# Reordering the head, the block change and the last group of a two-layer feed-forward kernel

## The chip, the cores and the metric

The kernel runs on one core of one Trainium2 chip. The metric is the device time of one execution in microseconds (us). The times given are those of three runs.

## What is computed

```python
# x: (4, 512, 512) = 2048 tokens of 512 values, all float32
# layer 1 (weights 1376 x 512), keeps the larger half of |silu(gate)| of every token
s = silu(ln(x) @ w_gate.T)
s[the 688 smallest |s| of each row] = 0
x = x + ln((s * (ln(x) @ w_up.T)) @ w_down.T)
# layer 2, the same without the selection
x = x + ln((silu(ln(x) @ W_gate.T) * (ln(x) @ W_up.T)) @ W_down.T)
```

`ln` is a layer norm without scale and shift.

## The kernel before

The kernel is written with one instruction list for each engine; the order within a list is fixed by hand and engines wait for each other through semaphores only. TensorE (PE) multiplies, ScalarE (ACT), VectorE (DVE) and GpSimd (POOL) do the rest, and SyncE (SP) issues all DMAs.

**Precision.** Every matrix product is made of three matmuls. Each operand is split into a rounded part `hi` (made by ScalarE, `split_..._hi`) and the rest `lo` (made by VectorE, `split_..._lo`); the three are hi x lo, lo x hi and hi x hi.

**First block (layer 1).** The 2048 tokens are 16 tiles of 128. For tile j PE makes three gate products of 460 columns (`product(j, 0, n)`), three up products (`product(j, 1, n)`), each of 12 matmuls, and later the down product `down(j)` of 11 chunks of h, 33 matmuls of 512 columns, in three groups of chunks (4, 4, 3: `TG`), for each of which it waits for its part of the split h (`hlo_done`). The gate and up products rotate through five, later seven PSUM banks. A bank is free for the next product when ScalarE's `silu(j, n)` (gate) or VectorE's `times_up(j, n)` (up) has read it.

**Selection.** Between silu and the down product of a tile stands a chain over four engines: VectorE takes absolute values (`abs_values`), ScalarE counts six times how many exceed a threshold (`count(j, 0)` to `count(j, 5)`), GpSimd moves the threshold after each of the first five (`newton`), VectorE looks for the exact limit (`find_below`, `find_top`, `find_flag`), masks (`select`) and turns h (`swap_h`), a DMA of four parts moves it (`move_h`), then `split_h_hi` on ScalarE and `split_h_lo` on VectorE split it in three groups each. `down(j - 2)` stands among the products of tile j. `y_stats`, `y_rstd` (GpSimd), `normalise_y` (ScalarE) and `add_residual` (VectorE) finish a tile.

**Weights of the first block** come in 18 pieces (`PIECES`): 6 of gate, 6 of up (number 11 is the second half of the third up product), 6 of down with two chunks each (numbers 12 to 17). ScalarE and VectorE split each (`split_weights_hi`, `split_weights_lo`). `wlo_done` counts the pieces that are done; `NP` is 18 and `GU_PIECES` is 12.

**Second block (layer 2).** The tokens are four groups of four tiles (`GROUPS`, `GT`). Products are turned: `chunk(g, j, m)` makes gate (m = 0) or up (m = 1) of 128 rows of the hidden layer for 512 tokens, 12 matmuls, for 11 chunks j (`JC`). The weights are loaded into the buffers of the first block in pairs of chunks (`split_pair_hi`, `split_pair_lo`); the first pair of gate and that of up serve chunks 0 and 1. `down2(g, j, tiles)` adds chunk j to the y of the given tiles, 3 matmuls for each tile, and each of the four tiles has its own bank. In the last group `down2` of the last three chunks stands behind the last `chunk`.

The lists meet at these places, all of which the change touches: PE's `down`, the chunks of the block change (line 622) and the last group (lines 636 to 647); ScalarE's list of the head (lines 779 to 786) and its tile loop (line 813); VectorE's tile loop (line 1170) and its last lines (1270 to 1274).

Of the kernel before, what the change touches and what calls it, by code (L numbers as in the profile page):

```python
# [16 lines left out]
def sandwich(nc, x, x_first, w_gate, w_up, w_down, W_gate, W_up, W_down, out):  # L17
# [5 lines left out]
    JC = -(-I // P)  # L23
# [8 lines left out]
    GT = 4  # L32
    GROUPS = TILES // GT
# [64 lines left out]
    with ctx:  # L98
# [375 lines left out]
        def _(pe):  # L474
# [46 lines left out]
            def down(j):  # L521
                if j >= 1:
                    pe.wait_ge(res_done, j)
                if j == 0:
                    pe.wait_ge(wlo_done, NP)
                    pe.wait_ge(xlo_done, 4)
                for g, (c0, cn) in enumerate(TG):
                    pe.wait_ge(hlo_done, 3 * j + g + 1)
                    for c in range(c0, c0 + cn):
                        hhi, hlo = (hT[:, s, c * P:(c + 1) * P] for s in range(2))  # L530
                        for i, (h, w) in enumerate(((hhi, down_lo), (hlo, down_hi), (hhi, down_hi))):
                            last = nc.tensor.matmul(y_ps[:, :], h, w[:, c, :],  # L532
                                                    start=(c == 0 and i == 0),
                                                    stop=(c == JC - 1 and i == 2))
                last.then_inc(y_done, 1)

            def chunk(g, j, m):

                idx = g * JC + j
                what = ("gu"[m], idx, 0)  # L540
                bank_free(what)
                if g == 0:
                    pe.wait_ge(plo_done, P_AT[m * NPAIR + j // 2])
                if j == 0 and m == 0:
                    pe.wait_ge(xlo_done, POS[TILES + GT * g + GT - 1] + 1)
                dst = bank(what)
                k = width(j)
                xt = x_group(g)
                for c in range(KC):
                    at = j * KC * P + c * k  # L550
                    hi, lo = gu_hi[m][:, at:at + k], gu_lo[m][:, at:at + k]
                    for i, (w, s) in enumerate(((lo, 0), (hi, 1), (hi, 0))):
                        last = nc.tensor.matmul(dst[0:k, :], w, xt[:, s, c, :],  # L553
                                                start=(c == 0 and i == 0), stop=(c == KC - 1 and i == 2))
                last.then_inc((g2_done, u2_done)[m], 1)
# [63 lines left out]
                    if n == max(6 - j, 0) and j < TILES - 1:  # L619
                        down(j - 2)  # L620
            down(TILES - 3)
            for j in range(2):
                chunk(0, j, 0)
                chunk(0, j, 1)
            down(TILES - 2)
            for j in range(2, 4):
                chunk(0, j, 0)
# [7 lines left out]
            for g in range(GROUPS):  # L635
                for j in range(6 if g == 0 else 0, JC):
                    chunk(g, j, 0)
                    chunk(g, j, 1)
                    if g > 0 and j == 0:
                        down2(g - 1, JC - 1, range(GT))  # L640
                    if j >= 2:
                        down2(g, j - 2, range(GT))
                if g < GROUPS - 1:
                    down2(g, JC - 2, range(GT))
            for r in range(GT):
                down2(GROUPS - 1, JC - 2, (r,), last_tile=False)
                down2(GROUPS - 1, JC - 1, (r,))

        @block.scalar
        def _(act):  # L650
            def split_weights_hi(w):
                m, n, c = PIECES[w]
                slot = w % NSLOT
                act.wait_ge(stage_in[slot], 16 * (w // NSLOT + 1))
                if m < 2:
                    src = stage[:, slot, :, 0:CW[n]]
                    dst = gu_hi[m][:, :].rearrange("p (c i) -> p c i", c=KC)[:, c:c + 2, CO[n]:CO[n] + CW[n]]
                else:
                    src, dst = stage[:, slot, 0:c, :], down_hi[:, n:n + c, :]
                nc.scalar.activation(dst, src, ACT.Copy).then_inc(whi_done, 1)  # L660
# [35 lines left out]
            def silu(j, n):  # L696
                act.wait_ge(g_done, G_AT[j, n])
                if j >= 2:
                    act.wait_ge(h_moved, 64 * (j - 1))
                nc.scalar.activation(prod[:, j % 2, CO[n]:CO[n] + CW[n]], bank(("G", j, n))[:, 0:CW[n]],  # L700
                                     ACT.Silu).then_inc(silu_done, 1)
# [77 lines left out]
            silu(1, 1)  # L779
            split_weights_hi(10)  # L780
            silu(1, 2)
            count(0, 2)
            split_weights_hi(11)
            count(0, 3)
            split_weights_hi(12)
            count(0, 4)
# [24 lines left out]
            split_x_hi(4)  # L811
            split_h_hi(1)
            for j in range(3, TILES - 1):
                count(j - 1, 5)
                silu(j, 0)
                if j > 3:
                    split_h_hi(j - 2)
                silu(j, 1)
                silu(j, 2)
                if j - 1 in TWO:  # L820
                    split_x_hi(TILES + j - 1 - TWO[0])
                if 4 < j < TWO[0]:
                    split_x_hi(j + 1)
                guess(j)
                for n in range(3):
                    count(j, n)
                if j in TWO:
                    split_x_hi(j + 1)
                count(j, 3)
                normalise_y(j - 2)  # L830
                count(j, 4)
                if j == 3:
                    split_x_hi(5)
# [61 lines left out]
        def _(dve):  # L895
# [274 lines left out]
            for j in range(3, TILES - 1):  # L1170
                a = XSEQ[POS[j + 1]:]
                find_below(j - 1)
                find_top(j - 1)
                if j > 3:
                    split_h_lo(j - 2)
                abs_values(j)
                if j - 1 in TWO:
                    split_x_lo(TILES + j - 1 - TWO[0])
                if 4 < j < TWO[0]:
                    split_x_lo(j + 1)  # L1180
                if j > 3:
                    x_stats(a[1])
                find_flag(j - 1)
                select(j - 1)
                if j > 3:
                    x_normalise(a[1])
                swap_h(j - 1)
                if j in TWO:
                    split_x_lo(j + 1)
                    x_stats(a[2])  # L1190
                y_stats(j - 2)
                times_up(j, 0)
                if j in TWO:
                    x_normalise(a[2])
                add_residual(j - 2)
                times_up(j, 1)
                times_up(j, 2)
                if j == 3:
                    split_x_lo(5)
            last = TILES - 1  # L1200
# [43 lines left out]
            for g in range(GROUPS):  # L1244
                for j in range(4 if g == 0 else 0, JC):
# [18 lines left out]
                    if g < GROUPS - 1:  # L1264
                        if j in X_AT:
                            split_x_lo(a + X_AT[j])
                        if j + 1 in X_AT:
                            x_stats(a + X_AT[j + 1])
                            x_normalise(a + X_AT[j + 1])
            for r in range(GT):  # L1270
                y_stats(XT2 - GT + r)
                if r:
                    add_residual(XT2 - GT + r - 1)
            add_residual(XT2 - 1)

        @block.gpsimd
# [147 lines left out]
```

## Time and profile before

| | us |
|---|---|
| median of three runs (749.35 to 749.54) | 749.38 |
| the profiled execution | 748.73 |
| its span in the trace | 746.9 |
| PE busy | 733.0 |
| VectorE busy | 448.0 |
| ScalarE busy | 345.9 |
| GpSimd busy | 133.2 |

Times in the trace count from the start of the span. TensorE's granted clock was 0.997 of full speed over the span. In the order of time of an engine a line gives the start, the length, the engine, the line of the kernel, the operation, what it writes and reads, how many like instructions are merged in the line, and in brackets the idle time of the engine before it with what ended it. Matmuls overlap, so the length of one is more than the distance to the next. "L969" is VectorE's split of h, "L918" its split of a weight piece, "L1007" `times_up`, "L930" its split of a pair, "L1101" and "L1108" the product and the split of h in the second block.

### The profile page before, as it was taken

Reading aid. Unit: us, or ns where it says so; the run is one execution under the profiler, and the core shown is the slowest. Engines: PE = TensorE matmul, PEld = TensorE weight load, DVE = VectorE, ACT = ScalarE, POOL = GpSimd, SP = SyncE. Lnnn points to the kernel's source line nnn. Section 1 sums busy time; section 2 is a strip of 40 time slices with the busy share of each in tenths; the row PEclk is TensorE's granted clock in tenths of the full one; section 3 lists DMA queues with packets and bytes.
Section 4 is the critical chain, followed back from the end, with each engine's and each line's share of the span. In section 5 each row is a group of like instructions: output and inputs, shape, how many; then the busy total and the mean of one; then the engine's idle time right before and its main releaser. Section 6 shows DMA issues by size and latency. Waiting matters only on the chain.

```text
span 746.9 us, 9447 instructions
## 1 busy us (share of the span) xinstructions
PE 733.0 (98%) x3309; PEld 615.7 (82%) x3309; DVE 448.0 (60%) x865; ACT 345.9 (46%) x575; POOL 133.2 (18%) x278
## 2 busy tenths in 40 slices
PE   8999999999999999999999999999999999999996
PEld 7888878888888888888788887888878888788884
DVE  7788778888787788887876452533316333151214
ACT  6786676776666676667735221311113112131112
POOL 0432123233322223332210000100001000010001
PEclk9999999999999999999999999999999999999998
DMA  8532235544335554557726112111112122030001
GB/s 285 185 88 69 64 105 134 132 109 89 110 96 133 147 113 103 126 143 215 269 74 204 32 29 57 73 41 29 33 53 85 28 37 34 15 134 8 1 1 56
DMA packets 88610, 69.85 MB, mean 94 GB/s; under 512 B 60368, under 2 KB 72144, under 8 KB 88368
## 3 DMA queue, kind: packets, MB, share of 16 engines
q1 hardware_dynamic: 88560, 69.23, 34.0%
q8 instruction: 26, 0.43, 0.2%
q14 instruction: 24, 0.20, 0.1%
HBM read 42.21 MB, written 16.84 MB: 79 GB/s over the span
## 4 chain that ended last, share of the span: by engine, by line
PE 68%; DVE 11%; issue 9%; POOL 5%; ACT 5%; DMA 1%; DVEq 0%; POOLq 0%; SPq 0%; ACTq 0%
PE gu_ps L553 32%; PE tr_ps L574 12%; PE y_ps L532 8%; PE gu_ps L517 7%; PE tr_ps L517 5%; PE y_ps L574 4%; ACT junk L688 3%; POOL move L1319 2%; POOL thr L1322 2%; DVE below L1051 2%; DVE hT L969 2%; DVE top L1056 1%; DVE xstat L937 1%; DVE absv L1000 1%; DMA xin<-in_x_first 1%
## 5 line engine op out<-in xcount | busy, mean ns | idle before, releaser
L688 ACT ACTIVATE junk<-absv,thr 128x1383 bf16<-128x1383 f32 x96 | 139.2, 1450 | 52.3 <-POOL thr L1322 51.6
L1101 DVE TENSOR_TENSOR prod<-gu_ps,prod 128x512 f32<-128x512 f32 (+1 forms) x44 | 30.3, 689 | 166.8 <-PE gu_ps L553 166.5
L532 PE MATMUL y_ps<-down_hi,hT 128*128 128x512 f32 x352 | 109.0, 391 | 0.0
L741 ACT ACTIVATE prod<-gu_ps 128x512 f32<-128x512 f32 (+1 forms) x44 | 26.2, 595 | 132.1 <-PE gu_ps L553 132.1
L532 PEld LDWEIGHTS y_ps<-down_hi,hT 128*128 128x128 f32 x352 | 66.1, 188 | 14.4
L532 PE MATMUL y_ps<-down_lo,hT 128*128 128x512 f32 x176 | 69.5, 395 | 1.6 <-DVE hT L969 1.1
L517 PE MATMUL gu_ps<-up_hi,xT 128*128 128x460 f32 (+1 forms) x240 | 69.5, 371 | 0.0
L517 PE MATMUL gu_ps<-gate_hi,xT 128*128 128x460 f32 (+1 forms) x232 | 67.2, 371 | 0.0
L1319 POOL TENSOR_SCALAR move<-sgn 128x1 f32<-128x1 f32 x80 | 40.1, 502 | 94.0 <-ACT junk L688 93.8
L1303 POOL TENSOR_TENSOR yrstd<-yvar,half 128x1 f32<-128x1 f32 x32 | 18.7, 583 | 208.1 <-DVE yvar L978 207.2
L553 PE MATMUL gu_ps<-xg_odd,gate_hi 128*128 128x512 f32 (+1 forms) x176 | 54.4, 390 | 0.0
L553 PE MATMUL gu_ps<-xg_even,gate_hi 128*128 128x512 f32 (+1 forms) x176 | 54.3, 390 | 0.0
L553 PE MATMUL gu_ps<-xg_even,up_hi 128*128 128x512 f32 (+1 forms) x176 | 54.3, 390 | 0.0
L553 PE MATMUL gu_ps<-xg_odd,up_hi 128*128 128x512 f32 (+1 forms) x176 | 54.3, 389 | 0.0
L1296 POOL TENSOR_TENSOR xrstd<-xvar,half 128x1 f32<-128x1 f32 x32 | 19.1, 595 | 187.3 <-DVE xvar L941 187.3
L517 PEld LDWEIGHTS gu_ps<-up_hi,xT 128*128 128x128 f32 x240 | 45.1, 188 | 5.2
L517 PEld LDWEIGHTS gu_ps<-gate_hi,xT 128*128 128x128 f32 x232 | 43.6, 188 | 4.9
L517 PE MATMUL gu_ps<-up_lo,xT 128*128 128x460 f32 (+1 forms) x120 | 44.8, 373 | 0.5 <-DVE prod L1007 0.5
L755 ACT ACTIVATE xT<-prod 128x512 fp32r<-128x512 f32 (+1 forms) x22 | 13.9, 632 | 67.1 <-DVE prod L1101 63.6
L517 PE MATMUL gu_ps<-gate_lo,xT 128*128 128x460 f32 (+1 forms) x116 | 43.4, 374 | 0.7 <-DVE gate_lo L918 0.4
L517 PE MATMUL tr_ps<-gate_hi,xT 128*128 128x460 f32 (+1 forms) x152 | 44.1, 371 | 0.0
L517 PE MATMUL tr_ps<-up_hi,xT 128*128 128x460 f32 (+1 forms) x144 | 41.7, 371 | 0.0
(137 smaller groups left out, 1527.2 us busy)
## 6 DMA issues: line engine op xcount, KB each, us to landing
absv<-prod SPq DMA_DIRECT2D x64, 176.0 KB, 3.4
xin<-x_scratch SPq DMA_DIRECT2D x18, 256.0 KB, 2.7
xres<-in_L_attn_x SPq DMA_DIRECT2D x16, 256.0 KB, 5.2
x_scratch<-xres SPq DMA_DIRECT2D x16, 256.0 KB, 2.8
xres<-x_scratch SPq DMA_DIRECT2D x14, 256.0 KB, 2.8
out<-xres SPq DMA_DIRECT2D x14, 256.0 KB, 2.1
xin<-in_L_attn_x SPq DMA_DIRECT2D x11, 256.0 KB, 3.5
xT<-xin SPq DMA_DIRECT2D x44, 64.0 KB, 2.5
```

Source lines behind the costliest of these rows:

```text
L517: last = nc.tensor.matmul(dst[:, 0:CW[n]], xt, w, start=(c == 0 and i == 0), stop=(c == KC - 1 and i == 2))
L532: last = nc.tensor.matmul(y_ps[:, :], h, w[:, c, :], start=(c == 0 and i == 0), stop=(c == JC - 1 and i == 2))
L553: last = nc.tensor.matmul(dst[0:k, :], w, xt[:, s, c, :], start=(c == 0 and i == 0), stop=(c == KC - 1 and i == 2))
L574: last = nc.tensor.matmul(y_bank(b)[:, :], h[0:k, toks], w[0:k, j, :], start=(j == 0 and i == 0), stop=(j == JC - 1 and i == 2))
L688: nc.scalar.activation(junk[:, 0:I + PAD], absv[:, q, A0 - PAD:A0 + I], ACT.Sign, bias=thr[:, q:q + 1], scale=-1.0, accum_out=sgn[:, q:q + ...
L741: nc.scalar.activation(prod[0:k, 0, 0:GW], bank(("g", idx, 0))[0:k, :], ACT.Silu).then_inc(s2_done, 1)
L969: nc.vector.tensor_tensor(lo, raw, hi.bitcast(F32), ALU.subtract).then_inc(hlo_done, 1)
L1051: nc.vector.scalar_tensor_tensor(below[:, :], values(q), thr[:, q:q + 1], values(q), ALU.is_le, ALU.mult).then_inc(below_done, 1)
L1101: nc.vector.tensor_tensor(prod[0:k, 0, GW:2 * GW], bank(("u", idx, 0))[0:k, :], prod[0:k, 0, 0:GW], ALU.mult).then_inc(p2_done, 1)
L1296: nc.gpsimd.tensor_tensor(xrstd[:, :], xvar[:, :], half[:, :], ALU.pow).then_inc(xr_done, 1)
L1303: nc.gpsimd.tensor_tensor(yrstd[:, q:q + 1], yvar[:, q:q + 1], half[:, :], ALU.pow).then_inc(yr_done, 1)
L1319: stepped(nc.gpsimd.tensor_scalar(move[:, :], sgn[:, q:q + 1], sgn[:, q:q + 1], float((WINDOW - 1) ** 2) + 0.5, ALU.mult, ALU.is_gt))
```

## The change

It moves work and removes or adds none, but for the waits of one product.

- `down(0)` waits for the weight pieces of each group of chunks instead of for all 18 at its start.
- At the change of blocks PE makes gate 0, gate 1, up 0, up 1 instead of gate 0, up 0, gate 1, up 1.
- In the last group, behind the last chunk, PE makes chunks 8 and 9 of tiles 0 and 1, then chunk 10 of tiles 0 and 1, then all three of tile 2 and all three of tile 3. Before, it made chunk 8 of all four tiles and then chunks 9 and 10 tile by tile.
- In the head ScalarE splits weight piece 11 ahead of the third count of tile 0.
- In the loop's tiles 4 to 10 ScalarE's `split_h_hi(j - 2)` stands ahead of the sixth count of tile j - 1, and VectorE's `split_h_lo(j - 2)` ahead of `find_top(j - 1)`. For tiles 11 on nothing moves.
- In the loop's tiles 3 to 5 VectorE's `add_residual(j - 2)` stands behind the third `times_up(j, n)` instead of the first.
- At the end VectorE takes the statistics of tiles 0, 1 and 2 before the first residual add, and those of tile 3 behind it.

```diff
                 if j == 0:
-                    pe.wait_ge(wlo_done, NP)
                     pe.wait_ge(xlo_done, 4)
                 for g, (c0, cn) in enumerate(TG):
+                    if j == 0:
+                        pe.wait_ge(wlo_done, GU_PIECES + (c0 + cn + 1) // 2)
...
             down(TILES - 3)
-            for j in range(2):
-                chunk(0, j, 0)
-                chunk(0, j, 1)
+            for m in range(2):
+                chunk(0, 0, m)
+                chunk(0, 1, m)
...
-                    if j >= 2:
+                    if j >= 2 and (g, j) != (GROUPS - 1, JC - 1):
                         down2(g, j - 2, range(GT))
...
-            for r in range(GT):
-                down2(GROUPS - 1, JC - 2, (r,), last_tile=False)
-                down2(GROUPS - 1, JC - 1, (r,))
+
+            for r, chunks in ((0, 2), (1, 2), (0, 1), (1, 1), (2, 3), (3, 3)):
+                for j in range(JC - 3, JC - 1) if chunks > 1 else ():
+                    down2(GROUPS - 1, j, (r,), last_tile=False)
+                if chunks != 2:
+                    down2(GROUPS - 1, JC - 1, (r,))
...
             silu(1, 2)
+            split_weights_hi(11)
             count(0, 2)
-            split_weights_hi(11)
             count(0, 3)
...
             for j in range(3, TILES - 1):
+                if 3 < j < TWO[0]:
+                    split_h_hi(j - 2)
                 count(j - 1, 5)
                 silu(j, 0)
-                if j > 3:
+                if j >= TWO[0]:
                     split_h_hi(j - 2)
...
                 find_below(j - 1)
+                if 3 < j < TWO[0]:
+                    split_h_lo(j - 2)
                 find_top(j - 1)
-                if j > 3:
+                if j >= TWO[0]:
                     split_h_lo(j - 2)
...
-                add_residual(j - 2)
+                if j > 5:
+                    add_residual(j - 2)
                 times_up(j, 1)
                 times_up(j, 2)
+                if j <= 5:
+                    add_residual(j - 2)
...
-            for r in range(GT):
-                y_stats(XT2 - GT + r)
-                if r:
-                    add_residual(XT2 - GT + r - 1)
+            y_stats(XT2 - 4)
+            y_stats(XT2 - 3)
+            y_stats(XT2 - 2)
+            add_residual(XT2 - 4)
+            y_stats(XT2 - 1)
+            add_residual(XT2 - 3)
+            add_residual(XT2 - 2)
             add_residual(XT2 - 1)
```

## Rows read from the trace of the kernel before

**Rows 1.** The page's first section: busy time, share and instructions of each engine.
```profile
PE 733.0 (98%) x3309; PEld 615.7 (82%) x3309; DVE 448.0 (60%) x865; ACT 345.9 (46%) x575; POOL 133.2 (18%) x278
```
**Rows 2.** Waits of PE: engine, tile, line, releaser: us in total, times, longest.
```profile
PE y_ps L532 <- DVE hT L969: 1.1, 3, 0.6
```
**Rows 3.** PE in order of time, tiles 0 to 6 of the first block.
```profile
33.04 0.58 PE L517 MATMUL tr_ps<-up_hi,xT 128*128 128x456 f32 x2
34.35 0.47 PE L517 MATMUL tr_ps<-up_lo,xT 128*128 128x456 f32 x1 [0.73 <-DVE up_lo L918]
...
56.68 0.37 PE L517 MATMUL tr_ps<-gate_lo,xT 128*128 128x460 f32 x1
...
59.88 0.50 PE L532 MATMUL y_ps<-down_lo,hT 128*128 128x512 f32 x1 [0.52 <-DVE down_lo L918]
...
80.53 0.43 PE L532 MATMUL y_ps<-down_lo,hT 128*128 128x512 f32 x1
...
98.89 0.48 PE L517 MATMUL gu_ps<-up_lo,xT 128*128 128x460 f32 x1 [0.54 <-DVE prod L1007]
...
104.46 0.47 PE L532 MATMUL y_ps<-down_lo,hT 128*128 128x512 f32 x1 [0.28 <-DVE hT L969]
...
145.97 0.47 PE L532 MATMUL y_ps<-down_lo,hT 128*128 128x512 f32 x1 [0.61 <-DVE hT L969]
```
**Rows 4.** Order of time at the change of blocks, PE and VectorE.
```profile
365.67 0.47 PE L553 MATMUL gu_ps<-xg_even,up_lo 128*128 128x512 f32 x1 [0.67 <-DVE up_lo L930]
...
390.28 1.28 DVE L969 TENSOR_TENSOR hT<-absv,hT 128x512 fp32r<-128x512 f32 x2
...
392.37 0.39 PE L532 MATMUL y_ps<-down_lo,hT 128*128 128x512 f32 x1
```
**Rows 5.** Order of time of the last group, PE, VectorE and SyncE.
```profile
732.98 0.69 DVE L1108 TENSOR_TENSOR hT<-prod,hT 96x512 fp32r<-96x512 f32 x1 [0.70 <-ACT hT L755]
...
739.30 0.63 PE L574 MATMUL y_ps<-down_hi,hT 96*128 96x512 f32 x2
...
741.02 0.69 DVE L974 BATCH_NORM_STATS2 ystat<-y_ps 128x6 f32<-128x512 f32 x1
...
744.27 0.81 SPq L373 DMA_DIRECT2D out<-xin  x2
```
**Rows 6.** Order of time of the head, GpSimd, ScalarE and VectorE.
```profile
27.64 2.76 POOL L1322 TENSOR_SCALAR thr<-move,step,thr 128x1 f32<-128x1 f32 x1
...
32.06 0.29 POOL L1319 TENSOR_SCALAR move<-sgn 128x1 f32<-128x1 f32 x1 [1.67 <-ACT junk L688]
...
32.47 0.34 POOL L1322 TENSOR_SCALAR thr<-move,step,thr 128x1 f32<-128x1 f32 x1
33.06 1.44 ACT L688 ACTIVATE junk<-absv,thr 128x1383 bf16<-128x1383 f32 x1
33.19 1.11 DVE L918 TENSOR_TENSOR up_lo<-stage,up_hi 128x912 fp32r<-128x912 f32 x1 [2.29 <-ACT up_hi L660]
```
**Rows 7.** Order of time of tiles 2 to 6, ScalarE and VectorE.
```profile
55.66 0.56 ACT L700 ACTIVATE prod<-tr_ps 128x460 f32<-128x460 f32 x1 [2.35 <-DMA absv<-prod]
...
79.66 1.75 DVE L969 TENSOR_TENSOR hT<-absv,hT 128x512 fp32r<-128x512 f32 x3
...
97.60 0.69 DVE L993 TENSOR_TENSOR xres<-y_ps,xres 128x512 f32<-128x512 f32 x1 [2.44 <-ACT y_ps L727]
98.21 1.17 DVE L1007 TENSOR_TENSOR prod<-gu_ps,prod 128x460 f32<-128x460 f32 x2
...
141.96 1.65 DVE L1051 SCALAR_TENSOR_TENSOR below<-absv,thr 128x1376 f32<-128x1376 f32 x1 [0.46 <-POOL thr L1322]
...
145.15 1.74 DVE L969 TENSOR_TENSOR hT<-absv,hT 128x512 fp32r<-128x512 f32 x3
```
**Rows 8.** The page's DMA issues: tiles, count, KB each, us from issue to landing.
```profile
absv<-prod SPq DMA_DIRECT2D x64, 176.0 KB, 3.4
xin<-x_scratch SPq DMA_DIRECT2D x18, 256.0 KB, 2.7
xres<-in_L_attn_x SPq DMA_DIRECT2D x16, 256.0 KB, 5.2
```

## The prediction before the run

> **What bounds the kernel now.** I read the page first: TensorE (PE) is busy 733.0 of 746.9 us [rows 1]. So only two things can be shortened by a change that removes no work: the idle time of PE, and what runs before its first and after its last matmul. The waits view of PE lists nine kinds of wait, 6.9 us in all; the largest after the start is the down product waiting for the split of h, 1.1 us in three waits [rows 2]. PE's own order of time then gives the place of each. A wait costs more than the idle figure, so I measure it as the start of the matmul against the start it would have had: matmuls of 460 columns start 0.21 us apart and those of 512 columns 0.23, and the first one after a wait takes 0.47 instead of 0.37 us, 0.10 more. The row pair at 33.04 and 34.35 us [rows 3] gives 34.35 - (33.04 + 0.42) = 0.89, and with the restart 0.99 us. In the same way: first down product at 59.88, 0.69 + 0.10; second up product of tile 4 at 98.89, 0.71 + 0.10; down products of tiles 2, 3 and 4 at 104.46, 125.06 and 145.97, 0.45, 0.36 and 0.78, each + 0.10 (the first and the last of the three stand there); the first up chunk of the second block at 365.67, 0.84 + 0.10 [rows 3, 4]. After 366 us PE waits for nothing that counts, until the tail: the last matmul ends at 739.93, the statistics of its tile start at 741.02, and the last two stores are issued from 744.27 on [rows 5].
>
> **Who is behind PE.** Most of the early waits are ends of one chain that PE does not drive: ScalarE counts, GpSimd moves the threshold, VectorE selects and turns h, a DMA moves it, ScalarE and VectorE split it. I call it the selection chain. A wait on PE that is removed only helps until PE next meets this chain; so I follow PE from gate to gate, with the gain G that it has against before.
>
> **Head: the split of piece 11 ahead of the third count.** That count waits for the threshold that GpSimd delivers at 27.64 + 2.76 = 30.40 [rows 6], and the change puts the 0.95 us split into this idle time, so it costs nothing on ScalarE. VectorE's half (1.11 us, at 33.19) has 2.29 us of idle time before it, so it can start at 33.19 - 2.29 = 30.90 and is done about 31.95 instead of 34.30 [rows 6]. PE's third up product wants it at 33.46: the wait is gone, G = 0.99. The fourth count no longer stands behind the split: it started at 33.06 and its threshold was ready at 32.47 + 0.34 = 32.81, so it can start at about 32.85 [rows 6]. The whole selection chain moves 0.21 us forward.
>
> **Gate 1, tile 3's first gate product.** It was at 56.68 without a wait; its bank is freed by the silu at 55.66, 0.56 long, which waits for the DMA that moves h [rows 3, 7]. With G = 0.99 PE wants the bank at 55.69, and the silu ends at 56.22 - 0.21 = 56.01. A new wait of about 0.4 us with restart: G falls to about 0.5.
>
> **Gate 2, the first down product.** Its first four chunks need pieces 12 and 13 of down and the first part of split h, both done at about 58; the piece it waited for, which VectorE finished just before 59.88 [rows 3], is now asked for with the last chunks, 5.5 us later. The wait of 0.79 goes: G = 1.3. Nothing is queued behind the two waits that the change adds on PE but its own matmuls, and their semaphores are long up.
>
> **Gate 3, the second down product.** It started at 80.53 [rows 3], and the first of the three splits it needs ends about 0.7 after 79.66, at 80.35 [rows 7]. It had no slack at all. The change reorders nothing here, so this gate moves by the chain's 0.21 only, less a restart: G = 0.15. Nearly all that the head and the first down product gave is handed back. This is the step that a sum of removed waits would miss.
>
> **Tile 4's up product.** The residual add of tile 1 waited for the normalised y with 2.44 us idle, and the two VectorE products behind it at 98.21 held PE's bank [rows 7]. With the add behind them they need not wait and PE has its bank: 0.81 more, G = 0.96. The add itself still ends near 98.1, with the next down product 5 us away.
>
> **Down products of tiles 2, 3 and 4.** Before, VectorE did below (1.65), top, then the split, which started 3.19 us after below (141.96, 145.15) [rows 7]. Now the split comes between, 1.6 us sooner, if ScalarE's half is there. That half now stands ahead of the sixth count; it takes 1.56 us and waits for the h DMA, whose last part lands about 3.4 to 3.9 us after its issue [rows 8], which is 0.5 us after ScalarE comes free in tiles 5 and 6. It pushes the sixth count and the first silu back by some 1.6 to 2.1 us; the third silu ends where VectorE is done with top, within 0.1 us, so abs and the next count start no later (chain at -0.47 to -0.52, since below, split, top and abs now follow without VectorE's small gaps). Then, by the same steps in VectorE's order of time: down 2 is ready at 102.6 and wanted at 103.06 (104.02 without its wait, less 0.96), G = 1.5. Down 3 is ready at 122.9 and wanted at 123.2, G = 1.96. Down 4: below starts at 141.96 - 0.47, the first split ends at 143.73, PE starts 0.14 later at 143.87; it would have wanted 143.23. One wait of 0.64 stays, and G = 145.97 - 143.87 = **2.10**. The three down products stand (145.97 - 104.46) / 2 = 20.8 us apart because the chain sets them; a tile of PE is 72 x 0.21 + 33 x 0.23 = 22.7. From down 5 on, behind whole tiles, PE does not meet the chain again, and from tile 9 the third silu waits for PE, so the chain follows at -2.1. Bounds for this part: 1.6 if the chain does not move at all (only the reorder counts), 2.7 if the last wait goes too.
>
> **Change of blocks.** Gate chunk 0, gate chunk 1, up chunk 0, up chunk 1: the up weights are wanted 2.7 us later than before, and they were 0.84 late [rows 4]. Gate chunk 1 needs the same pair of gate weights as chunk 0 and a bank that was freed by a silu of the last tile, long before. Total **0.94**. What is next: the split of h for down 15. It starts at 390.28, its first part takes 0.68 and PE takes it up 0.14 later, at 391.1; PE asked at 392.37 and will ask at 391.44 [rows 4]. It keeps 0.3 us of cover. Bounds 0.8 to 0.94.
>
> **Tail.** In the last group PE does two chunks of two tiles first, then their last chunks, then tile 2 and tile 3 with three chunks each; twelve groups of 0.70 us as before. The last chunk's h is split at 732.98 + 0.69 = 733.67 [rows 5] and is now wanted at 734.2 instead of 734.9: 0.5 us of cover is left where it was 1.2. Tile 2 ends at 737.8 instead of 738.5, and VectorE does its statistics (1.1), the add of tile 0, and is free at 739.6, before the last matmul's end at 739.93. The last statistics start at 739.97 instead of 741.02: 1.05 earlier, and GpSimd, ScalarE and the two half adds follow (the other adds fit before the half add at 742.8). The stores come closer together: those of tiles 1 and 2 and the two halves would be issued about 0.6, 0.9 and 0.4 us apart, where each of the halves was clear of the others before. I take **1.0**, bounds 0.5 (transfers get in each other's way) to 1.05.
>
> **Sum.** 2.10 + 0.94 + 1.0 = 4.04 us. The profiled execution took 748.73 with a span of 746.9, so it would go to 744.7 and 742.9; the median of the runs shown is 749.38, so **745.3**.
>
> **Rivals.** (a) Every wait goes and nothing is late next: 0.99 + 0.79 + 0.81 + 0.55 + 0.46 + 0.88 + 0.94 + 1.05 = 6.5, 742.9. Against it stands gate 3 without slack. 6%. (b) The selection chain does not move or gets longer by about 1 us, and the tail gives half: GpSimd's operation took 2.76 us where its like take 0.34, under two VectorE operations that read SBUF [rows 6]. Should the moved split (to 31.95) overlap the next one at 32.06, the chain loses up to 1.1 us: 4.04 - 1.1 = 2.9, down to 2.0 with the tail at 0.5 less and a little more waiting, 746.5 to 747.4. 20%. The Trainium skill (GPSIMD Engine Reference, Specifications) says that the SBUF interfaces are shared with VectorE and that instructions with two SBUF inputs contend; by that rule this edit is safe only by the 0.1 us between the two, and the time would be 746.4. (c) The change doesn't do what it says: down 2 to 4 are late by the DMA instead of by the order and the tail is held by the stores; gain under 1.5, about 748.5. 8%. (d) Slower: ScalarE's half of the split, now ahead of the sixth count, waits for the h DMA in tiles 4 to 10. If this lands 2 us later than now in tiles 4 to 6 (the residual load needs 5.2 us to land where this one needs 3.4 [rows 8]), sixth count, silus and abs of each tile slip by 2 us, three times 2 against the 4 gained: about 751. It decides from 1.9 us of delay on; now it is 0.5. 4%. The forecast has 62%.
>
> **Range and chances.** The forecast's own bounds are 1.6 + 0.8 + 0.5 = 2.9 to 2.7 + 0.94 + 1.05 = 4.7, 744.7 to 746.5; with most of (b) and half of (a) the range is 743.7 to 747.0. 0.2% (1.5 us) is about what can be told from no change: faster by more 0.88, within 0.08, slower 0.04.
>
> **What would show it.** Right: no wait at 33, 59, 98, 103 and 123 us; new small waits near 56 and 80; one of 0.6 left before down 4; none at 364; span near 742.9; last statistics 0.05 us after the last matmul. Wrong: PE's gain at down 1 much over 0.2 would mean that the chain moved more than I think; a longer idle time of PE at down 4 than 0.8, that ScalarE's new order lengthens the chain; a long GpSimd operation at 32 us, rival (b).

## The result and the profile after

The changed kernel takes 745.11 us (median of four runs, 744.72 to 745.35) against 749.37 before (749.35 to 749.54): 4.26 us less, ratio 0.9942 with an interval of 0.993 to 0.9953. Forecast were 745.3 us and a gain of 4.04. The interval allows a gain of 3.5 to 5.2 us, so that the two agree to 0.2 us is closer than the runs can tell. The profiled execution of after is its slowest, 745.35, with a span of 743.5.

The first section of the page, then the waits of PE (us in total, times, longest):

```profile
span 743.5 us, 9449 instructions
PE 731.9 (98%) x3309; PEld 616.0 (83%) x3309; DVE 446.9 (60%) x865; ACT 345.0 (46%) x575; POOL 132.7 (18%) x278
```
```profile
PE y_ps L533 <- DVE hT L975: 1.2, 2, 1.0
PE tr_ps L517 <- ACT prod L704: 0.7, 1, 0.7
```

Busy times are those of before [rows 1] to within 1.1 us. The three waits of the down products [rows 2] have become two, and a wait for a silu is new. PE's own order of time gives their places:

```profile
56.91 0.48 PE L517 MATMUL tr_ps<-gate_lo,xT 128*128 128x460 f32 x1 [0.72 <-ACT prod L704]
...
81.20 0.47 PE L533 MATMUL y_ps<-down_lo,hT 128*128 128x512 f32 x1 [0.98 <-DVE hT L975]
...
98.90 0.37 PE L517 MATMUL gu_ps<-up_lo,xT 128*128 128x460 f32 x1
...
103.92 0.39 PE L533 MATMUL y_ps<-down_lo,hT 128*128 128x512 f32 x1
...
124.06 0.40 PE L533 MATMUL y_ps<-down_lo,hT 128*128 128x512 f32 x1
...
144.56 0.47 PE L533 MATMUL y_ps<-down_lo,hT 128*128 128x512 f32 x1 [0.22 <-DVE hT L975]
...
366.13 0.39 PE L554 MATMUL gu_ps<-xg_even,up_lo 128*128 128x512 f32 x1
```

The brackets at 34, 59, 98, 104, 125 (0.21) and 365 us of before [rows 3, 4] are gone. Those at 56.91 and 81.20 stand where the forecast put new ones, and a small one stays ahead of the fifth down product (down 4). Where the residual add was moved, VectorE now does it at 98.30, behind both products. VectorE's split of h (L975) follows `below` directly, and ScalarE's half stands ahead of the sixth count and waits for its DMA:

```profile
121.97 1.57 ACT L725 ACTIVATE hT<-absv 128x512 fp32r<-128x512 f32 x3 [1.12 <-DMA absv<-prod]
```
```profile
142.16 1.65 DVE L1057 SCALAR_TENSOR_TENSOR below<-absv,thr 128x1376 f32<-128x1376 f32 x1 [1.54 <-POOL thr L1336]
143.72 1.75 DVE L975 TENSOR_TENSOR hT<-absv,hT 128x512 fp32r<-128x512 f32 x3
```

The tail of after; it answers to [rows 5]:

```profile
736.92 0.62 PE L575 MATMUL y_ps<-down_hi,hT 96*128 96x512 f32 x2
737.25 2.42 SPq L368 DMA_DIRECT2D out<-xres  x2
...
737.58 0.70 DVE L980 BATCH_NORM_STATS2 ystat<-y_ps 128x6 f32<-128x512 f32 x1 [0.36 <-PE y_ps L575]
...
739.92 0.33 SPq L368 DMA_DIRECT2D out<-xin  x1
...
740.83 0.83 SPq L373 DMA_DIRECT2D out<-xin  x2
```

The last matmul ends at 737.54 (736.92 + 0.62), 2.39 earlier than before, and the last statistics start 0.04 behind it. The span is shorter by 3.4, so 1.0 comes from behind the last matmul. These 3.4 are less than the 4.26 of the medians; the next part of the trace tells why.

**The head, where the two profiled executions differ.** GpSimd and ScalarE of after, then VectorE's statistics of x tile 3 in before, after and the first experiment:

```profile
26.79 1.36 POOL L1310 TENSOR_TENSOR xrstd<-xvar,half 128x1 f32<-128x1 f32 x1 [2.44 <-DVE xvar L947]
28.14 0.29 POOL L1333 TENSOR_SCALAR move<-sgn 128x1 f32<-128x1 f32 x1
28.54 2.76 POOL L1336 TENSOR_SCALAR thr<-move,step,thr 128x1 f32<-128x1 f32 x1
32.97 0.29 POOL L1333 TENSOR_SCALAR move<-sgn 128x1 f32<-128x1 f32 x1 [1.67 <-ACT junk L692]
```
```profile
31.34 1.45 ACT L692 ACTIVATE junk<-absv,thr 128x1383 bf16<-128x1383 f32 x1 [2.49 <-POOL thr L1336]
...
33.75 1.45 ACT L692 ACTIVATE junk<-absv,thr 128x1383 bf16<-128x1383 f32 x1 [0.55 <-POOL thr L1336]
```
```profile
24.69 0.70 DVE L937 BATCH_NORM_STATS2 xstat<-xin 128x6 f32<-128x512 f32 x1 [0.90 <-DMA xin<-in_x_first]
```
```profile
25.61 0.69 DVE L943 BATCH_NORM_STATS2 xstat<-xin 128x6 f32<-128x512 f32 x1 [1.47 <-DMA xin<-in_x_first]
```
```profile
26.10 0.69 DVE L938 BATCH_NORM_STATS2 xstat<-xin 128x6 f32<-128x512 f32 x1 [1.93 <-DMA xin<-in_x_first]
```

The same x tile lands 0.92 later in after. Its reciprocal root stands in GpSimd's list ahead of the second threshold step, which thus runs at 28.54 instead of 27.64 [rows 6]. In all nine profiled kernels with this order of the head (24.69 to 26.10 for the statistics) the step starts 2.93 to 2.95 us behind them. The third count follows at 31.34 and the whole selection chain runs 0.7 later than in the trace of before (0.9, less the 0.2 that the new order gives). The change did not cause this: the first experiment below, an execution of 749.93 us where its median is 749.21, shows still more of it. Over the nine kernels the time of the profiled execution less the kernel's median rises, on the whole, with the start of these statistics: -0.64 and -0.55 us at 24.69 and 24.96, 0.03 at 25.45, 0.24 and 0.72 at 25.61 and 26.10. The execution of before on which the forecast was made (748.73) was likewise an early one against its median of 749.38.

### The profile page after: what moved, and what is told of

The parts are those of the page before. It is cut to its first block, busy times and chain, and to the rows that moved or that the text cites. A ratio compares the mean times of both kernels' runs of the same rounds, so it can differ in the third digit from the quotient of the medians.

```text
span 743.5 us, 9449 instructions
## 1 busy us (share of the span) xinstructions
PE 731.9 (98%) x3309; PEld 616.0 (83%) x3309; DVE 446.9 (60%) x865; ACT 345.0 (46%) x575; POOL 132.7 (18%) x278
## 4 chain that ended last, share of the span: by engine, by line
PE 80%; issue 6%; DVE 5%; ACT 4%; POOL 3%; DMA 1%; SPq 0%; DVEq 0%; POOLq 0%; ACTq 0%
PE gu_ps L554 32%; PE tr_ps L575 12%; PE y_ps L533 12%; PE gu_ps L517 11%; PE tr_ps L517 8%; PE y_ps L575 4%; ACT junk L692 2%; POOL move L1333 1%; POOL thr L1336 1%; DVE below L1057 1%; DVE hT L975 1%; DVE absv L1006 1%; DMA absv<-prod 1%; POOL xrstd L1310 0%; DVE xstat L943 0%
```

## Experiments

Each kernel was timed in five rounds beside the kernel before on the same chip. The edits are made to the kernel before unless the heading says another.

**The split of piece 11 ahead of the third count, and the first down product's waits, alone.**

```diff
-                    pe.wait_ge(wlo_done, NP)
+                        pe.wait_ge(wlo_done, GU_PIECES + (c0 + cn + 1) // 2)
...
+            split_weights_hi(11)
             count(0, 2)
-            split_weights_hi(11)
```


> Only the two edits of the head: the split of piece 11 ahead of the third count, and the down product of tile 0 that waits for its own pieces. Theory of the gates (prediction): both waits of PE go (0.99 and 0.79 us), but the second down product had no slack behind the selection chain, so 0.15 to 0.25 us are left of it at 80 us, and the waits at 98 to 146 us come back as they were: gain 0.2 us, ratio 0.9997. Rival, sum of removed waits: 1.8 us, ratio 0.9976.

749.21 against 749.41 us, ratio 0.9997 (0.9988 to 1.0006). Both waits are gone from the trace, and two others, longer ones, stand further on:

```profile
57.50 0.48 PE L517 MATMUL tr_ps<-gate_lo,xT 128*128 128x460 f32 x1 [1.30 <-ACT prod L701]
...
81.71 0.47 PE L533 MATMUL y_ps<-down_lo,hT 128*128 128x512 f32 x1 [0.92 <-DVE hT L970]
```

Two removed waits of 0.99 and 0.79 us are worth 0.2 us, by the interval at most 0.9: PE runs up against the selection chain. The reading by gates holds, the sum of waits (1.8) does not.

**The moved splits of h and residual adds, alone.**

```diff
+                if 3 < j < TWO[0]:
+                    split_h_hi(j - 2)
                 count(j - 1, 5)
...
+                if 3 < j < TWO[0]:
+                    split_h_lo(j - 2)
                 find_top(j - 1)
...
+                if j <= 5:
+                    add_residual(j - 2)
```


> Only the edits of tiles 3 to 10: h is split ahead of the sixth count and of top, and the residual add of tiles 1 to 3 goes behind the third product. Gates: the down product of tile 4 is set by the selection chain, whose split comes 1.6 us sooner, and the chain gains 0.3 from VectorE's small gaps: gain 1.9 us, ratio 0.9975; PE's wait before the down product of tile 3 or 4 does not vanish. Rival, sum of removed waits: 0.81 + 0.55 + 0.46 + 0.88 = 2.7 us. Rival (d), the chain gets longer by the wait for the DMA: no gain or a loss.

747.47 against 749.41, ratio 0.9973 (0.9961 to 0.9984). As by the gates: the waits at 34 and 59 us are there (34.62, 60.16), those from 98 to 125 are not, and before down 4, at 144.14, 0.39 is left without the restart (idle 0.22).

**The order of the first two chunks, alone.**

```diff
-            for j in range(2):
-                chunk(0, j, 0)
-                chunk(0, j, 1)
+            for m in range(2):
+                chunk(0, 0, m)
+                chunk(0, 1, m)
```


> Only the new order of the first four chunks of the second block. All theories: 0.94 us, ratio 0.9987, and no wait of PE near 364 us. If a wait before the down product of tile 15 or the first down product of the second block takes it back, the gain is 0.3 us or less.

748.43 against 749.41, ratio 0.9987 (0.9978 to 0.9996): the 0.94 of the forecast.

**The last group, alone** (PE's part and VectorE's as in the change; the lines show where each begins to differ).

```diff
+            for r, chunks in ((0, 2), (1, 2), (0, 1), (1, 1), (2, 3), (3, 3)):
...
+            y_stats(XT2 - 2)
+            add_residual(XT2 - 4)
+            y_stats(XT2 - 1)
```


> Only the last group: PE's order and VectorE's. Prediction: the last statistics start 0.05 us after the last matmul instead of 1.1, gain 1.0 us, ratio 0.9987. Rival, stores in each other's way: 0.5 us, with the last store landing over 2 us after its issue.

748.62 against 749.41, ratio 0.9989 (0.998 to 0.9999): 0.8 where 1.0 was forecast, and the interval holds both. The four parts alone give 0.2 + 1.94 + 0.98 + 0.79 = 3.9 of the 4.26.

**The last group, only VectorE's order.**

```diff
-            for r in range(GT):
-                y_stats(XT2 - GT + r)
...
+            y_stats(XT2 - 2)
+            add_residual(XT2 - 4)
+            y_stats(XT2 - 1)
```


> The kernel before with VectorE's order at the end alone (statistics of tile 2 ahead of the first residual add), PE's order as before. Tile 2 ends at 738.5, its statistics take 1.1, the add of tile 0 0.7, so the last statistics start at 740.3 instead of 741.0: gain 0.7 us of the tail's 1.05, ratio 0.9991. If VectorE's order does nothing without PE's: 0.

748.73 against 749.52, ratio 0.9991 (0.9982 to 1.0). VectorE's order alone brings about what the whole part did (0.79 each). In the traces the last statistics start 1.09 us behind the last matmul in before, 0.29 with VectorE's order and 0.03 with both; that last 0.26 is below what these intervals tell.

**Only the residual adds, and only the splits of h** (the two halves of the second experiment).

```diff
-                add_residual(j - 2)
+                if j > 5:
+                    add_residual(j - 2)
                 times_up(j, 1)
                 times_up(j, 2)
+                if j <= 5:
+                    add_residual(j - 2)
```


> Only the residual adds of tiles 1 to 3 behind the third product. PE's wait at 98.9 us (0.81) goes, but the down product of tile 2 is set by the chain and comes when it came before, about 0.1 us sooner at most: gain 0.1 to 0.2 us, ratio 0.9998. Sum of removed waits: 0.8 us, 0.9989.

749.52 against 749.61, ratio 1.0001 (0.9991 to 1.001).

```profile
98.90 0.37 PE L517 MATMUL gu_ps<-up_lo,xT 128*128 128x460 f32 x1
...
105.22 0.47 PE L532 MATMUL y_ps<-down_lo,hT 128*128 128x512 f32 x1 [1.14 <-DVE hT L969]
```

The wait at 98 us is gone, and the down product 6 us on waits 1.14 instead of 0.28 [rows 3]: a removed wait of 0.81 is worth nothing by itself.

```diff
+                if 3 < j < TWO[0]:
+                    split_h_hi(j - 2)
                 count(j - 1, 5)
...
+                if 3 < j < TWO[0]:
+                    split_h_lo(j - 2)
                 find_top(j - 1)
```


> Only the split of h ahead of the sixth count and of top in tiles 4 to 10. The down products of tiles 2 to 4 have their data 1.6 us sooner each; PE's wait at 98.9 us stays, and so PE wants down 4 at 145.2 less the waits at 104 and 125 (0.55, 0.46), 144.2, while the chain offers it at 144.2: gain 1.7 us, ratio 0.9977. Together with the residual edit 2.0 were measured; a sum of both parts alone of 2.0 or less would agree.

747.73 against 749.61, ratio 0.9973 (0.9962 to 0.9983).

```profile
99.71 0.48 PE L517 MATMUL gu_ps<-up_lo,xT 128*128 128x460 f32 x1 [0.59 <-DVE prod L1009]
...
145.06 0.39 PE L532 MATMUL y_ps<-down_lo,hT 128*128 128x512 f32 x1
```

Nearly the whole gain of the tiles is this one edit, because it moves the last gate at which PE meets the chain.

**After, with x of tile 3 prepared later.** If the chain sets what PE can win, freeing it of the x tile's landing must help.

```diff
             x_normalise(2)
-            x_stats(3)
             split_weights_lo(9)
-            x_normalise(3)
...
             split_weights_lo(11)
+            x_stats(3)
             times_up(1, 0)
             times_up(0, 1)
+            x_normalise(3)
             split_weights_lo(12)
...
-            newton(0, 0)
+            for n in range(3):
+                newton(0, n)
             x_rstd(3)
-            for n in range(1, STEPS):
+            for n in range(3, STEPS):
```


> The changed kernel, and in the head the statistics and the normalisation of x tile 3 (which PE transposes only at 48 us) stand later: VectorE's behind the split of piece 11 and the first products, GpSimd's reciprocal root behind the third threshold step instead of ahead of the second. In the traces the second step stands behind it and so waits for a DMA that landed at 24.7 us before and 25.6 after. Theory of the gates: the third count starts about 2 us sooner, the whole selection chain follows, and PE's waits at 56, 80 and 144 us (0.98, 1.25 and 0.49 with restart) go or shrink: gain 2 to 2.7 us on the changed kernel, 742.4 to 743.1, ratio to the kernel before 0.991. Rival, the chain is bound elsewhere (a GpSimd step held up under VectorE's operations on SBUF): at most 0.9 us, ratio 0.993.

744.68 against 749.61, ratio 0.9934 (0.9921 to 0.9948). That is 4.93 us below its own before, where after is 4.26 below: about 0.7 better, where 2 and more were expected, and the two intervals overlap. The rival of the expectation (at most 0.9) is what came. GpSimd, then ScalarE, then VectorE:

```profile
27.48 0.33 POOL L1336 TENSOR_SCALAR thr<-move,step,thr 128x1 f32<-128x1 f32 x1
31.41 0.29 POOL L1333 TENSOR_SCALAR move<-sgn 128x1 f32<-128x1 f32 x1 [3.60 <-ACT junk L692]
31.82 1.21 POOL L1336 TENSOR_SCALAR thr<-move,step,thr 128x1 f32<-128x1 f32 x1
```
```profile
29.78 1.45 ACT L692 ACTIVATE junk<-absv,thr 128x1383 bf16<-128x1383 f32 x1
...
33.07 1.45 ACT L692 ACTIVATE junk<-absv,thr 128x1383 bf16<-128x1383 f32 x1 [1.42 <-POOL thr L1336]
...
35.79 1.44 ACT L692 ACTIVATE junk<-absv,thr 128x1383 bf16<-128x1383 f32 x1
```
```profile
31.72 1.10 DVE L924 TENSOR_TENSOR up_lo<-stage,up_hi 128x912 fp32r<-128x912 f32 x1
```

The second threshold step takes 0.33 instead of 2.76 and the third count starts 1.56 earlier, but the third step meets VectorE's split of piece 11 and takes 1.21: the fourth count (33.07) is only 0.68 earlier. That is the gain, and it is rival (b)'s mechanism, one step further on. Two more things kept the third count from coming sooner: the first step (24.06) now falls under another split and takes 1.34 instead of 0.39, and ScalarE works through its list until 29.78 although the threshold is there at 27.81. PE's wait at 56 us is gone; that before the second down product stays, 0.91 idle at 80.53.

**The kernel before with x of tile 3 later.** The same edit as above.

```diff
-            x_stats(3)
...
+            x_stats(3)
```


> The kernel before with the same edit alone (x tile 3 prepared later, no other edit). If the selection chain sets every wait of PE from 80 to 146 us, the gain is what the chain gains, about 2 us, ratio 0.9973, with no edit at any of these waits. If the waits have causes of their own, the gain is 0.2 us or less.

748.46 against 749.61, ratio 0.9984 (0.9975 to 0.9994): 1.15 us, between the two forecasts.

```profile
35.56 1.46 ACT L688 ACTIVATE junk<-absv,thr 128x1383 bf16<-128x1383 f32 x1 [0.78 <-POOL thr L1322]
```

The waits before the down products of tiles 2, 3 and 4 keep their size (idle 0.30, 0.20 and 0.60 against 0.28, 0.21 and 0.61) while the products start 0.21 to 0.24 earlier than in the trace of before, and so does this fifth count (35.77 there): these waits move with the chain. PE's wait at 34 us is gone too. The size was off for another reason than in the kernel above. No split held the third step (31.59, 0.34); its comparison took 0.84 beside the absolute values, and the root of x tile 3, at 34.00, stands ahead of the fourth step. The rest of the 1.15 is not shown in steps; the trace of before was an early execution by 0.64.

**The product of tile 1 ahead of the split of piece 11** (made to the kernel with x of tile 3 later).

```diff
+            times_up(1, 0)
             split_weights_lo(11)
             x_stats(3)
-            times_up(1, 0)
```


> The kernel of x3_later (changed kernel, x tile 3 prepared later), with one more move in the head: VectorE takes the first up product of tile 1, which reads PSUM, ahead of the split of piece 11, which reads two SBUF tensors. In the trace of x3_later that split ran at 31.72 to 32.82 us and GpSimd's threshold step beside it took 1.21 us (31.82 to 33.03) instead of 0.34, and held the fourth count. Theory, GpSimd is held up under such an operation, and the selection chain sets the time: the fourth count starts 0.8 us sooner and the time falls by 0.7 to 0.9 us from x3_later. Rival, the long step has another cause, or the chain no longer sets the time: 0.2 us or less.

745.73 against 749.52, ratio 0.9953 (0.9939 to 0.9967): the forecast fell, it is 1 us slower than the kernel it is made from (745.39 to 746.53 against 744.41 to 744.93, on two chips).

```profile
31.87 0.34 POOL L1336 TENSOR_SCALAR thr<-move,step,thr 128x1 f32<-128x1 f32 x1
34.51 0.56 POOL L1310 TENSOR_TENSOR xrstd<-xvar,half 128x1 f32<-128x1 f32 x1 [2.30 <-DVE xvar L947]
35.06 0.30 POOL L1333 TENSOR_SCALAR move<-sgn 128x1 f32<-128x1 f32 x1
35.46 1.46 POOL L1336 TENSOR_SCALAR thr<-move,step,thr 128x1 f32<-128x1 f32 x1
```
```profile
35.10 0.55 DVE L952 TENSOR_SCALAR xin<-xin,xmv,xrstd 128x512 f32<-128x512 f32 x1
35.56 1.22 DVE L924 TENSOR_TENSOR down_lo<-stage,down_hi 128x1024 fp32r<-128x1024 f32 x1
```

The step that was aimed at is down to 0.34. But the root of x tile 3 now holds up the next one, which falls under the normalisation of this x tile and the split of piece 12, and the fifth count starts at 36.95 instead of 35.79.

**Further splits moved out of the way, tiles 1 and 2** (made to the kernel of products first).

```diff
             count(1, 4)
+            count(1, 5)
             silu(2, 0)
             split_h_hi(0)
-            split_weights_hi(17)
-            count(1, 5)
             silu(2, 1)
             silu(2, 2)
+            split_weights_hi(17)
...
+            find_below(1)
+            find_top(1)
+            split_h_lo(0)
             split_weights_lo(15)
+            abs_values(2)
             split_weights_lo(16)
-            find_below(1)
-            split_h_lo(0)
             split_weights_lo(17)
-            find_top(1)
-            abs_values(2)
```


> The kernel of products_first, with the same idea at 53 us: the splits of pieces 15, 16 and 17 no longer stand ahead of the search of tile 1 on VectorE (15 goes ahead of, 16 and 17 behind the absolute values of tile 2), and ScalarE's sixth count of tile 1 goes ahead of the first silu of tile 2, whose DMA it waits for. GpSimd's step there took 2.35 us under two splits. The down product of tile 0 asks for these pieces by groups only since the change. Theory: the absolute values of tile 2 end about 1.2 us sooner, PE's wait before the second down product (1.17 in x3_later) goes, and the time falls by 1.0 to 1.2 us from products_first, to about 742.7 in a series whose kernel before takes 749.5. If the down product of tile 0 now waits for pieces 15 to 17, PE shows it near 61 to 64 us; this costs nothing up to 1 us. Rival, PE meets the chain elsewhere: 0.3 us or less.

746.25 against 749.52, ratio 0.9959 (0.9945 to 0.9973): the forecast fell again.

```profile
54.45 0.29 POOL L1333 TENSOR_SCALAR move<-sgn 128x1 f32<-128x1 f32 x1 [1.67 <-ACT junk L692]
...
62.91 1.70 POOL L1326 TENSOR_SCALAR unit<-gains,asum 128x5 f32<-128x5 f32 x1 [7.72 <-DVE absv L1006]
```

The comparison (`move`) of this step took 2.35 beside two splits in the kernel it is made from (at 54.28) and takes 0.29 here, and the absolute values of tile 2 end 1.2 us sooner (62.80 against 64.02), as expected. But the two splits put behind `abs_values` run from 62.73 to 64.55 and fall on GpSimd's next operation, 1.70 instead of 0.27, which takes this back, and PE's wait before the second down product is 1.41 against 1.01 in the kernel this one is made from.

**Thresholds first** (made to the kernel of products first). From the two failures: it isn't enough to move the split; GpSimd's list must let the step run in the window that is free.

```diff
-            for n in range(3):
+            for n in range(4):
                 newton(0, n)
             x_rstd(3)
-            for n in range(3, STEPS):
+            for n in range(4, STEPS):
```


> The version with x of tile 3 prepared later and the product of tile 1 ahead of the split of piece 11, and in it GpSimd's fourth threshold step of tile 0 ahead of the reciprocal root of x tile 3. In the version without that last step the fourth count ended at 33.78 us, but GpSimd sat in the root's wait (34.51 to 35.07), so that its step ran at 35.46, under VectorE's split of piece 12, and took 1.46 us; the fifth count started at 36.95. Now the two operations can run at 33.9 to 34.6, beside statistics and a product that read SBUF once. My theory (the selection chain sets the waits, and GpSimd's step is 0.34 us where no VectorE operation with two SBUF inputs runs beside it): step 0.34 us, fifth count at about 35.0 behind ScalarE's half of piece 12, which is 0.8 us sooner than in the best version so far (35.79) and 2.0 sooner than in the one it is made from; the time is 743.8 to 744.2, ratio 0.9923 to 0.993. Rival (each shift only moves the collision to another step, as it did in the last two versions): another GpSimd step of more than 1 us is seen between 35 and 66 us that was not there before, and the time stays at 744.7 or above, ratio 0.9935 and more.

743.85 us (743.54 to 744.07) against 749.55, ratio 0.9925 (0.9911 to 0.9938), as expected: the fastest kernel of the study, 5.7 us below before. Against the kernel with x of tile 3 later (4.93 below) the intervals overlap, the executions do not (that one's fastest took 744.41).

```profile
34.13 0.29 POOL L1333 TENSOR_SCALAR move<-sgn 128x1 f32<-128x1 f32 x1 [1.67 <-ACT junk L692]
34.54 0.33 POOL L1336 TENSOR_SCALAR thr<-move,step,thr 128x1 f32<-128x1 f32 x1
34.83 0.56 POOL L1310 TENSOR_TENSOR xrstd<-xvar,half 128x1 f32<-128x1 f32 x1
```
```profile
79.94 0.47 PE L533 MATMUL y_ps<-down_lo,hT 128*128 128x512 f32 x1 [0.34 <-DVE hT L975]
```

The fourth step is at 0.33, no other step between 35 and 66 us has become long (the 2.34 at 52.54 is after's 2.35 at 53.79), and the fifth count starts 5.13 us behind the third (35.22 - 30.09) instead of 6.01 (35.79 - 29.78). PE's wait at 56 us is gone and that at 80 us is 0.34 where after has 0.98.

## Why the prediction was right, and by which steps

- **Gates instead of a sum: right, and shown.** New waits at 56 and 81 us took the place of those removed at 34 and 59; the head alone brought 0.2 us and the residual adds alone nothing. The sum of removed waits (6.5 us) would have been 2.2 too much.
- **The chain moves 0.21 forward in the head: right in the order, not seen in the pair of traces.** After's fourth count starts at 33.75, 0.03 behind its threshold (32.97 + 0.29, then 0.34 from 33.38), and not behind the split as in before (33.06 against 32.81 [rows 6]). But its third count was already 0.9 late by the x tile's landing. That landing was not in the forecast at all: it took one execution's 24.69 as if it were the kernel's. Every gate came later than the forecast, by 0.69 to 0.96, about what the landing gives: PE at 56.91 (forecast 56.18), 81.20 (80.38), 103.92 (102.96), 124.06 (123.10), 144.56 (143.87). Taken as the forecast takes it, with restart, the wait at gate 1 is therefore 0.97 instead of 0.4. That at gate 3 is 1.24, which is not "small" but is what the forecast's own G says (from 1.3 to 0.15); it is 0.91 idle even where the chain does not wait for the landing (80.53 with x of tile 3 later).
- **Down products 2 and 3 without a wait, one before down 4: right in place.** That wait was forecast at 0.64 and is 0.39 by the same measure, from the start that PE would have had, without restart (idle 0.22), as PE also came later. At down 4 PE is 145.97 - 144.56 = 1.41 ahead in the pair of traces, not 2.10. The missing 0.7 is the chain's delay above. That the medians differ by 4.26, not by the spans' 3.4, fits this reading and the nine kernels above, but no run repeats one kernel at two landings, so the split of the 4.26 over the gates is inferred. One reading of the forecast was wrong and carried nothing: the down products of tiles 2 to 4 stand 20.8 us apart not because the chain sets them. Each stands one up product (12 x 0.21 = 2.5 us) earlier in PE's list than the one before it, which makes 20.2 of PE's own work, and the waits are the rest.
- **Change of blocks: right.** PE's lead grows from 1.43 at the first gate chunk to 2.36 at the down product behind the four chunks, by 0.93 (forecast 0.94), and the edit alone measured 0.98. Down 15, behind the next four chunks, starts at 390.00 without a wait.
- **Tail: right.** 1.0 in the pair of traces; alone 0.8. The stores, closer together, did not get in each other's way enough to show. That VectorE's order does most of it had not been said; PE's order adds 0.26 in the traces, which is below what the times can tell.
- **Rival (b) was close, and its mechanism is real.** In after VectorE's split of piece 11 (31.72, 1.10 long, as in the trace above) ends before GpSimd's move at 32.97, so nothing collides. With the third count 1.56 earlier the same split did hold the step, for 1.21. The 0.1 us of distance that the forecast named was 0.15 here (32.97 - 32.82).
- **Rivals (c) and (d): not seen.** ScalarE's half of the split does wait for its DMA (1.12 us at 121.97), but it did not lengthen the chain: in the second experiment, with the x tile's landing 0.27 later than in before, `below` of tile 5 starts at 141.74 against 141.96 [rows 7], which is the 0.5 that the forecast had for this order. Down 2 and 3 don't wait.

## What to carry to other kernels

Follow the saturated engine from one meeting with the next-slowest chain to the next, and count only the gain that it still has at the last of them; the edit that moves that gate is worth the gain, those at earlier gates next to nothing alone. Before a trace is taken as the kernel's, look how much of it hangs on when a transfer happened to land. When a small operation on a chain is long in one place and short elsewhere, ask what runs beside it, and place it, not only its neighbour.

## What the runs showed of the hardware

- **GpSimd's threshold operation of 128 x 1 takes 0.33 us, and 1.21 to 2.76 beside a VectorE operation with two inputs in SBUF.** It ends 0.05 to 0.21 behind that operation's end: 33.03 against 32.82 with x of tile 3 later, 36.92 against 36.78 with the product first. Several such operations in a row hold it through all of them (2.76 in the head of after, 28.54 to 31.30: a normalisation of x from 28.19, the split from 28.65, the absolute values from 29.67 to 31.25). VectorE's normalisation of x, whose one large input and output lie in SBUF, holds it too (VectorE, then GpSimd, in after):

```profile
134.12 0.53 DVE L952 TENSOR_SCALAR xin<-xin,xmv,xrstd 128x512 f32<-128x512 f32 x1
```
```profile
134.38 0.49 POOL L1336 TENSOR_SCALAR thr<-move,step,thr 128x1 f32<-128x1 f32 x1
```

An operation of VectorE that reads PSUM and SBUF, as `times_up` does, did not hold it (0.34 at 33.38 in after, beside 32.74 to 33.92), and neither does a split that starts behind it (GpSimd, then VectorE, in after):

```profile
51.78 0.34 POOL L1336 TENSOR_SCALAR thr<-move,step,thr 128x1 f32<-128x1 f32 x1
```
```profile
51.98 1.21 DVE L924 TENSOR_TENSOR down_lo<-stage,down_hi 128x1024 fp32r<-128x1024 f32 x1
```

Where the trace has the step start 0.10 ahead of the split and it is held all the same (35.46 against 35.56), it starts inside a normalisation (35.10 to 35.65). The Trainium skill (SBUF — State Buffer, SBUF: two separate sides) has the pair of ports as an exclusive lock for the whole instruction, which goes to whichever starts first; the waits of GpSimd in these traces agree with both.
- **The landing of one 256 KB tile in the head** varied from 24.7 to 26.1 us between the profiled kernels with the same order up to there. The two fastest kernels do not wait for it, and their five executions each lie within 0.53 us (744.41 to 744.93 and 743.54 to 744.07), where nine of before on the same chip as the last lie within 0.86 (748.9 to 749.76). That the landing makes the spread is not shown: the kernel of products first does not wait for it either, and its five lie within 1.14.
- **The first transposes on PE** (of the identity, as filler) came in two forms with a granted clock of 1.00 in both, the long one in six of the fourteen profiled kernels: ten matmuls of 128 columns in 1.26 us in after, in 2.34 in the kernel with x of tile 3 later.

```profile
6.56 1.26 PE L585 MATMUL y_ps<-ident 128*128 128x128 f32 x10
```
```profile
6.77 2.34 PE L585 MATMUL y_ps<-ident 128*128 128x128 f32 x10
```

The idle time ahead of them does not choose: it was 0.74 us in this kernel and 0.77 in the one with only the splits of h, which had the short form. The fastest kernel had the long form too, and what chooses stays open. It cost next to nothing: PE reaches the third up product at 32.63 with x of tile 3 later and at 32.57 in after.
